# A decoder layer in which VectorE takes two instructions of the cross-attention in the other order

## The chip, the cores and the metric

The kernel runs on one core of a Trainium2 chip. The metric is the device time of one execution in microseconds (us). Three runs of the kernel before took 3787.0, 3793.76 and 3797.38 us; their median is 3793.76 us.

## The reference

One decoder layer over x of 16 batches x 224 rows x 512, all in fp32. Three parts are added to x one after the other, each computed from a layer norm of x:

```python
x = x + self_attention(layernorm(x))          # 16 heads of 64, causal, rotary
x = x + cross_attention(layernorm(x), ctx)    # 16 heads of 32, 750 context rows of 384 a batch
x = x + experts(layernorm(x))                 # 8 experts, top 2, capacity 560 rows each, F = 2048
```

The change lies in the cross-attention:

```python
q = (x @ Wq).reshape(B, N, 16, 32);  k, v = (context @ Wk), (context @ Wv)   # likewise in heads
scores = einsum('bhid,bhjd->bhij', q, k) * 32 ** -0.5    # a mask over the 750 keys
out = einsum('bhij,bhjd->bhid', softmax(scores), v)      # then all heads side by side
return out @ Wo                                          # added to x: the "residual" below
```

## The kernel before, in words

The layer runs in three stages: self-attention, cross-attention, experts. Within a stage each engine has a program of its own, a fixed list of instructions that it takes strictly in this order; engines wait for one another by semaphores. No planner sorts them: the order stands in the code.

**Steps and sub-steps.** The cross-attention goes through 16 batches; batches 2 to 14 are a loop, the first two and the last are written out. A batch has four steps (g = 0 to 3), one for each group of four heads, and a step has four sub-steps (j = 0 to 3), one a head. In each sub-step PE (TensorE) computes the scores of 112 rows (half h = 0) against all keys, then some other work (`first_gap`), then the scores of the other 112 rows (h = 1), then more other work (`second_gap`). VectorE takes the row maximum of each (L1605, `maximum`), followed by its own `first_gap` and `second_gap`. The scores are computed a second time with the maximum subtracted, for the step before (L1170), ScalarE takes the exponential (L1440), POOL sums it (L1029 to L1035), PE multiplies by the values (L1183).

**Units and banks.** The other work comes in units: a projection or a transposition that fills one bank of PSUM, from which another engine takes the result. Three banks (`x_pj`) are handed out in turn in the order of a written list. For a whole batch it has 45 units; those of step g = 2 are

```python
"K30 M1_2 O1 K31 V14 V15 C00 C10 Q0 C20 M0_2 C01 Q1 C11"
```

so O1 and V15 share a bank (three places apart), as do K31 and C00, and each must wait until the unit ahead of it in its bank has been taken out (`pj_free`). The units that matter here:
- **K30, K31**: the keys of the next group of heads, columns 0 to 373 and 374 to 749. ScalarE writes a rounded ("high") copy (L1383), VectorE the difference ("low" part, L1599, `low_k`); a product of high and low parts then takes three matmuls (L32 to L34). When both parts of both halves are there, SP copies them into the stationary tiles `k_st` with three or four transfers a head (L953 to L957, `place_k`).
- **O0, O1**: the output projection of the batch before, 112 rows each (L1123). VectorE adds it to the residual `x_xres` (L1629, `residual`).
- **V14, V15**: parts of the values (L32 to L34 with `wv`, 9 matmuls each), taken out by ScalarE (L1387).
- **C00, C10**: transpositions of the next batch's context (L1089).
- **M0, M1**: the transposed maxima, written into partitions 96 to 98 of `q_st` by ScalarE (high) and VectorE (low, L1611, `low_max`).

**The place of the change** is step g = 2, sub-step j = 1, in VectorE's `second_gap`. PE's order there is: scores of j = 1 h = 0, K31, scores h = 1, sums of the exponentials (L1195), V14, V15, scores of j = 2. VectorE's order is: maximum h = 0, low part of M1_2, maximum h = 1, low part of K31, residual of O1, maximum of j = 2. SP's order is: the copies of K31's step (`place_k(t + 3, ...)`), the store of the finished residual, the queries of the next batch; later in the next body the context, the mask row and the keys of step 1.

Of the kernel before, what the change touches and what calls it, by code (L numbers as in the profile page):

```python
# [790 lines left out]
def unit_of(b, name):  # L791

    if isinstance(b, int) and b == -1:
        return Bank(U_PRE.index(name), 0, 0)
    start = len(U_PRE)
    if isinstance(b, int) and b == 0:
        return Bank(start + U_FIRST.index(name), 0, 0)
    start += len(U_FIRST)
    if isinstance(b, int) and b == 1:
        return Bank(start + U_SECOND.index(name), 0, 0)  # L800
    start += len(U_SECOND)
    if isinstance(b, int) and b == B - 1:
        return Bank(start + (B - 3) * len(UNITS) + U_LAST.index(name), 0, 0)
    return Bank(start - 2 * len(UNITS) + UNITS.index(name), b, len(UNITS))
# [20 lines left out]
def cross_attention(nc, x1, x1n, ctx, cmask, w_o, router_w, cst, x2, rows_w, logits, op):  # L825

    with ExitStack() as outer:
# [9 lines left out]
        with ExitStack() as c:  # L837
# [49 lines left out]
            def below(n, k):  # L887
                return isinstance(n, int) and n < k
# [17 lines left out]
            with nc.Block() as block:  # L906
# [660 lines left out]
                def _(dve):  # L1567
                    def any_key(b):

                        dve.wait_ge(mask_step, 3 * b + 1)  # L1570
                        dve.tensor_reduce(valid[:], mk[:], AX.X, ALU.max).then_inc(valid_done, 1)
# [4 lines left out]
                    def low_x(b, h):  # L1576
                        u, name = unit_of(b, f"X{h}"), f"X{h}"
                        hi_ready(b, name)
                        cols = slice(h * HT, (h + 1) * HT)
                        dve.tensor_tensor(xT[1][:, :, cols], pj[u.bank][:, 0:4 * HT].rearrange("p (k t) -> p k t", k=KD),  # L1580
                                          xT[0][:, :, cols].bitcast(F32), ALU.subtract).then_inc(pj_free[u.bank], 1)

                    def low_ctx(b, k, s):
                        u = unit_of(b, f"C{k}{s}")
                        hi_ready(b, f"C{k}{s}")
                        cols = slice(s * HALF, (s + 1) * HALF)
                        dve.tensor_tensor(cT[1][:, k, cols], pj[u.bank][:, 0:HALF], cT[0][:, k, cols].bitcast(F32),
                                          ALU.subtract).then_inc(pj_free[u.bank], 1)

                    def low_q(b, i):  # L1590
                        u = unit_of(b, f"Q{i}")
                        hi_ready(b, f"Q{i}")
                        dve.scalar_tensor_tensor(qT[1][:, i, :], pj[u.bank][:, 0:T], valid[:, 0:1], qT[0][:, i, :].bitcast(F32),
                                                 ALU.mult, ALU.subtract).then_inc(pj_free[u.bank], 1)
# [12 lines left out]
                    def low_max(u, n, g, i):  # L1607

                        dve.wait_ge(m_high, n)
                        rows = q_st[96:99, 4 * g + 2 * i:4 * g + 2 * i + 2, :]  # L1610
                        dve.scalar_tensor_tensor(rows, pj[u.bank][96:99, 0:2 * T].rearrange("p (j t) -> p j t", j=2),  # L1611
                                                 less[96:99, 0:1], rows.bitcast(F32), ALU.mult, ALU.add).then_inc(pj_free[u.bank], 1)

                    def invert(t, i):

                        dve.wait_ge(z_full, t + 1)
                        cols = slice(i * HT, i * HT + HT)
                        dve.reciprocal(rz[:, cols], psZ[:, cols]).then_inc(recip, 1)

                    def out_y(t, g, out=None):  # L1620
                        dve.wait_ge(recip, 2 * t + 2)
                        if out is not None:
                            dve.wait_ge(pj_full, out.n + 1)
                        dve.tensor_tensor(yT[:, g, :], psY, rz[:], ALU.mult).then_inc(y_ready, 1)

                    def residual(u, b, h):
                        dve.wait_ge(xres_loaded, 16 * b + 16)
                        dve.wait_ge(pj_full, u.n + 1)
                        dve.tensor_tensor(xres[:, h, :], pj[u.bank][0:HT, :], xres[:, h, :], ALU.add).then_inc(pj_free[u.bank], 1)  # L1629
# [35 lines left out]
                    def body(b, first, last):  # L1665
                        t = 4 * b
                        old = not below(b, 2)

                        def U(name):
                            return unit_of(b, name)  # L1670

                        def first_gap(g, j):
                            n, prev, pprev, gp = t + g, not (first and g == 0), not (first and g < 2), (g + 3) % 4
                            if j == 0:
                                if g == 1 and not last:
                                    low_x(b, 1)
                                elif g == 2 and not first:
                                    residual(U("O0"), b - 1, 0)
                            elif j == 1:
                                if prev:  # L1680
                                    low_max(U(f"M1_{g}"), 2 * n, gp, 1)
                            elif j == 2:
                                if pprev:
                                    invert(n - 2, 0)
                            else:
                                if g == 0:
                                    low_q(b, 3)
                                if pprev:
                                    out_y(n - 2, (g + 2) % 4, U("O1") if g == 2 and not first else None)
                                if g == 2 and not last:  # L1690
                                    low_ctx(b, 2, 0)
                                low_max(U(f"M0_{g}"), 2 * n + 1, g, 0)

                        def second_gap(g, j):
                            n, pprev = t + g, not (first and g < 2)
                            nxt, ng = not (last and g == 3), (g + 1) % 4
                            if j == 0:
                                if nxt:
                                    low_k(b, ng, 0)
                                if g == 3 and not last:  # L1700
                                    low_ctx(b, 2, 1)
                                if g == 3 and not first:
                                    router_norm(b - 1, 0, [U(f"O{h}") for h in range(2)])
                            elif j == 1:
                                if nxt:
                                    low_k(b, ng, 1)
                                if g == 2 and not first:
                                    residual(U("O1"), b - 1, 1)
                            elif j == 2:
                                if g == 0:  # L1710
                                    low_q(b, 2)
                                elif g == 2 and not last:
                                    low_ctx(b, 0, 0)
                                    low_ctx(b, 1, 0)
                                elif g == 3 and not first:
                                    router_norm(b - 1, 1)
                                if pprev:
                                    invert(n - 2, 1)
                                if g == 2 and not last:
                                    low_q(b, 0)  # L1720
                            else:
                                if g == 0 and not last:
                                    low_x(b, 0)
                                elif g == 1 and not last:
                                    any_key(b + 1)
                                elif g == 2 and not last:
                                    low_ctx(b, 0, 1)
                                    low_q(b, 1)
                                    low_ctx(b, 1, 1)
                                elif g == 3 and not first:  # L1730
                                    router_norm(b - 1, 2)

                        for g in range(4):
                            for j in range(4):
                                maximum(t + g, j, 0)
                                first_gap(g, j)
                                maximum(t + g, j, 1)
                                second_gap(g, j)
# [759 lines left out]
```

## Time and profile before

| | |
|---|---|
| median of three runs | 3793.76 us |
| the profiled execution | 3791.84 us, span 3790.1 us |
| PE busy | 3640.3 us, 96% of the span |
| PE's weight loads busy | 3139.0 us, 83% |
| VectorE busy | 2363.4 us, 62% |
| ScalarE busy | 1730.3 us, 46% |
| POOL busy | 1299.5 us, 34% |
| the cross-attention | from about 1090 to 2460 us |
| one batch of its loop | 83.7 us |

The span is the time from the first to the last instruction of one execution. A busy share is an average over stages; what an edit is worth is read from the waits of the stage in which it lies. PE is shown twice: its matmuls (PE) and the loading of their weights (PEld), which runs beside them and sets their pace here. An engine is idle ahead of an instruction either for want of something from another engine, which the profile names behind an arrow, or for "issue", where it names nothing. A line number is that of the kernel before.

### The profile page before, as it was taken

The numbers are of one execution on the slowest core, as the hardware profiler recorded it, in microseconds if no ns is written. First come the engines' busy times: TensorE is split into PE (matmuls) and PEld (weight loads), VectorE is DVE, ScalarE is ACT, GpSimd is POOL, SyncE is SP. The second block draws the span as 40 slices with busy tenths as digits, with TensorE's granted clock in tenths as the row PEclk, the third lists the DMA queues.
The fourth block names the chain that finished last, engine by engine and source line by source line (L and its number), as shares of the span: only waits on it lengthen the run. The fifth ranks groups of instructions, "written<-read, shape, count | busy, mean of one in ns | idle before, by whom it ended". The sixth has DMA issues, their size and how long they took to land. (4 is left out here: it accounts for less than half of the span.)

```text
span 3790.1 us, 84211 instructions
## 1 busy us (share of the span) xinstructions
PE 3640.3 (96%) x28244; PEld 3139.0 (83%) x28244; DVE 2363.4 (62%) x5547; ACT 1730.3 (46%) x4277; POOL 1299.5 (34%) x1385
## 2 busy tenths in 40 slices
PE   7999999999979999999999999849999999999999
PEld 6888888888868888888888888639999899989998
DVE  6888888888856666666666666567434334334343
ACT  4555555555535555555555555413333333333332
POOL 1333333333315556666555566510101101011010
PEclk9999999999979999999999999869999999999999
DMA  4222222222243443444434443223323333233232
GB/s 125 60 54 63 53 63 53 63 53 63 61 128 98 107 107 104 107 115 107 118 102 105 110 105 96 68 67 95 120 84 120 106 98 123 84 120 119 87 107 70
DMA packets 315057, 349.72 MB, mean 92 GB/s; under 512 B 45308, under 2 KB 232036, under 8 KB 314884
## 3 DMA queue, kind: packets, MB, share of 16 engines
q1 hardware_dynamic: 305796, 318.26, 30.3%
q0 software_dynamic: 9088, 29.17, 2.4%
q8 instruction: 106, 1.74, 0.2%
q14 instruction: 67, 0.55, 0.0%
HBM read 183.23 MB, written 38.91 MB: 59 GB/s over the span
## 5 line engine op out<-in xcount | busy, mean ns | idle before, releaser
L1605 DVE TENSOR_REDUCE x_mx<-x_psS 112x1 f32<-112x752 f32 x512 | 479.9, 937 | 388.3 <-PE x_psS L1158 384.5
L2401 DVE TENSOR_TENSOR hid<-e_psU,act_g 128x280 f32<-128x280 f32 x256 | 115.2, 450 | 626.2 <-PE e_psU L34 615.9
L1440 ACT ACTIVATE x_pt<-x_psE 125x448 f32<-125x448 f32 x768 | 389.2, 541 | 231.3 <-PE x_psE L1170 221.8
L1029 POOL TENSOR_TENSOR part<-x_pt 125x448 f32<-125x448 f32 x255 | 292.0, 1145 | 514.6 <-ACT x_pt L1440 505.8
L2027 POOL DMA_INDIRECT out<-ex_y,sidx x40 | 39.8, 994 | 1014.2 <-DVE ex_y L2435 1006.5
L611 POOL TENSOR_TENSOR qks<-qks,cos 128x448 f32<-128x448 f32 x128 | 147.8, 1155 | 676.6 <-DMA qks<-qk 676.6
L1158 PE MATMUL x_psS<-k_st,q_st 97*112 97x376 f32 x1024 | 287.5, 362 | 22.9 <-DMA k_st<-mk 15.0
L32 PE MATMUL e_psG<-ex_hi,g_hi 128*128 128x280 f32 x1024 | 303.9, 297 | 4.2 <-DVE ex_lo L2394 2.2
L32 PE MATMUL pj<-xT_hi,win_hi 128*128 128x224 f32 x1024 | 302.8, 296 | 1.4 <-DVE xT_lo L651 1.3
L32 PE MATMUL e_psU<-ex_hi,u_hi 128*128 128x280 f32 x1024 | 298.2, 291 | 0.4 <-DVE hid L2401 0.3
L1031 POOL TENSOR_TENSOR part<-part,x_pt 125x448 f32<-125x448 f32 x255 | 291.7, 1144 | 20.0
L34 PE MATMUL e_psG<-ex_hi,g_lo 128*128 128x280 f32 x1024 | 298.4, 291 | 0.0
L34 PE MATMUL e_psU<-ex_hi,u_lo 128*128 128x280 f32 x1024 | 297.7, 291 | 0.0
L33 PE MATMUL e_psG<-ex_lo,g_hi 128*128 128x280 f32 x1024 | 297.1, 290 | 0.0
L33 PE MATMUL e_psU<-ex_lo,u_hi 128*128 128x280 f32 x1024 | 297.0, 290 | 0.0
L2186 ACT ACTIVATE act_g<-e_psG 128x280 f32<-128x280 f32 x256 | 103.3, 404 | 423.5 <-PE e_psG L34 417.0
L34 PE MATMUL pj<-xT_hi,win_lo 128*128 128x224 f32 x1024 | 282.3, 276 | 0.0
L33 PE MATMUL pj<-xT_lo,win_hi 128*128 128x224 f32 x1024 | 281.7, 275 | 0.0
L1170 PE MATMUL x_psE<-q_st,k_st 99*125 99x224 f32 x1536 | 262.8, 280 | 6.4 <-ACT x_pt L1440 4.0
L1170 PEld LDWEIGHTS x_psE<-q_st,k_st 99*125 99x125 f32 x1536 | 235.9, 190 | 16.0 <-ACT x_pt L1440 11.6
L2190 ACT ACTIVATE hid_hi<-hid 128x280 fp32r<-128x280 f32 (+1 forms) x256 | 107.0, 418 | 288.5 <-DVE hid L2401 288.5
L674 DVE CUSTOM_DVE_ANT_0 pr<-psS,mask 112x112 f32<-112x112 f32 (+1 forms) x512 | 139.4, 329 | 128.8 <-issue 67.6
(301 smaller groups left out, 10888.3 us busy)
## 6 DMA issues: line engine op xcount, KB each, us to landing
k_st<-kT SPq DMA_DIRECT2D x768, 93.8 KB, 2.2
raw_g<-in_L_ffn_wg SPq DMA_DIRECT2D x128, 256.0 KB, 2.8
raw_u<-in_L_ffn_wu SPq DMA_DIRECT2D x128, 256.0 KB, 2.8
raw_d<-in_L_ffn_wd SPq DMA_DIRECT2D x128, 256.0 KB, 2.8
qks<-qk SPq DMA_DIRECT2D x512, 56.0 KB, 2.0
q_st<-qT SPq DMA_DIRECT2D x384, 56.0 KB, 2.0
ctxt<-in_ctx SPq DMA_DIRECT2D x16, 1125.0 KB
xt<-in_x SPq DMA_DIRECT2D x16, 448.0 KB, 3.7
```

What stands on the lines that cost most here:

```text
L32: pe.matmul(out, lh, rh, start=first, stop=False)
L33: pe.matmul(out, lh, rl, start=False, stop=False)
L34: return pe.matmul(out, ll, rh, start=False, stop=last)
L611: pool.tensor_tensor(qks[i][:], qks[i][:], cos[:].unsqueeze(1).to_broadcast((P, 2, T)), ALU.mult)
L674: m = dve.tensor_tensor_reduce(pr[par][:, hd, to:to + n], psS[hd][0:HT, to:to + n], mask[:, h, 0:n], -SD ** -0.5, -NEG, ALU.add, ALU.min, ...
L1029: pool.tensor_tensor(part[:], pt[j][:, 0, :], pt[j][:, 1, :], ALU.add).then_inc(parted, 1)
L1031: pool.tensor_tensor(part[:], part[:], pt[j][:, 2, :], ALU.add).then_inc(parted, 1)
L1158: m = pe.matmul(psS[0:HT, s, 0:376], q_st[0:97, head, h * HT:(h + 1) * HT], k_st[4 * (g % 2) + j][0:97, SHALF[s]], start=True, stop=True)
L1170: m = pe.matmul(psE[(j + i) % 2][0:KR, s * T:(s + 1) * T], k_st[4 * (g % 2) + j][0:99, r * KR:(r + 1) * KR], q_st[0:99, 4 * g + j, :], sta ...
L1440: act.activation(pt[j][:, i, :], psE[(j + i) % 2][0:KR, 0:2 * T], ACT.Exp, scale=XD ** -0.5).then_inc(exp_done, 1)
L1605: dve.tensor_reduce(mx[:, j, h:h + 1], psS[0:HT, :, 0:376], AX.XY, ALU.max).then_inc(s_taken, 1)
L2401: dve.tensor_tensor(h[ring][:, halves[s]], psU[:, 0:CH], act_g[i][:, halves[s]], ALU.mult).then_inc(S["mul"], 1)
```

## The change

In `second_gap` of VectorE, sub-step j = 1, the residual of O1 is placed ahead of the low part of the keys, not behind it. It concerns step g = 2 of batches 1 to 15; in the other steps only the low part is there. No other engine's program is touched, and no instruction is added or removed.

```diff
                             elif j == 1:
+                                if g == 2 and not first:
+                                    residual(U("O1"), b - 1, 1)
                                 if nxt:
                                     low_k(b, ng, 1)
-                                if g == 2 and not first:
-                                    residual(U("O1"), b - 1, 1)
                             elif j == 2:
```

## Rows read from the trace of the kernel before

**Rows 1.** The page: busy us (share of the span) and instructions of each engine.

```profile
PE 3640.3 (96%) x28244; PEld 3139.0 (83%) x28244; DVE 2363.4 (62%) x5547; ACT 1730.3 (46%) x4277; POOL 1299.5 (34%) x1385
```

**Rows 2.** One batch's length, busy PE, PEld, DVE, ACT, POOL; PEclk; DMA share, GB/s.

```profile
1560.00:1643.90 83.90, 82.54 (x718) 69.57 (x714) 56.32 (x82) 47.61 (x96) 49.98 (x62) 1.00 0.41 109
```

**Rows 3.** Waits of PE's weight loads, cross-attention: us in total, times, longest.

```profile
PEld x_pj L32 <- DVE x_xres L1629: 9.9, 15, 0.7
```

**Rows 4.** VectorE's timeline: start, us, line, operation, [idle before <- releaser].

```profile
1569.56 0.69 DVE L1611 SCALAR_TENSOR_TENSOR q_st<-x_pj,x_less,q_st 3x448 fp32r<-3x448 f32 x1
1571.15 0.94 DVE L1605 TENSOR_REDUCE x_mx<-x_psS 112x1 f32<-112x752 f32 x1 [0.89 <-PE x_psS L1158]
1572.12 0.55 DVE L1599 TENSOR_TENSOR kT<-x_pj,kT 128x376 fp32r<-128x376 f32 x1
1572.59 0.68 DVE L1629 TENSOR_TENSOR x_xres<-x_pj,x_xres 112x512 f32<-112x512 f32 x1
1575.04 0.94 DVE L1605 TENSOR_REDUCE x_mx<-x_psS 112x1 f32<-112x752 f32 x1 [1.77 <-PE x_psS L1158]
```

**Rows 5.** Timeline of PE's weight loads from V14 to V15.

```profile
1572.36 0.18 PEld L33 LDWEIGHTS x_pj<-wv,cT 128*125 128x125 f32 x1
1572.47 0.18 PEld L34 LDWEIGHTS x_pj<-wv,cT 128*125 128x125 f32 x1
1573.32 0.18 PEld L32 LDWEIGHTS x_pj<-wv,cT 128*125 128x125 f32 x1 [0.66 <-DVE x_xres L1629]
```

**Rows 6.** VectorE's timeline at O0's residual, batch 5 and (last two) batch 15.

```profile
1556.70 0.94 DVE L1571 TENSOR_REDUCE valid<-mk 128x1 f32<-128x750 f32 x1
1561.89 0.94 DVE L1605 TENSOR_REDUCE x_mx<-x_psS 112x1 f32<-112x752 f32 x1 [4.26 <-PE x_psS L1158]
1562.75 0.68 DVE L1629 TENSOR_TENSOR x_xres<-x_pj,x_xres 112x512 f32<-112x512 f32 x1
...
2399.28 0.94 DVE L1605 TENSOR_REDUCE x_mx<-x_psS 112x1 f32<-112x752 f32 x1 [5.22 <-PE x_psS L1158]
2400.25 0.69 DVE L1629 TENSOR_TENSOR x_xres<-x_pj,x_xres 112x512 f32<-112x512 f32 x1
```

**Rows 7.** Weight loads of C00 and C10, the next users of the two banks.

```profile
1575.19 0.65 PEld L1089 LDWEIGHTS x_pj<-ident,ctxt 125*128 125x128 f32 x6
```

**Rows 8.** SP's queue: copies of K31's step, queries, first copy of the next batch.

```profile
1572.94 0.51 SPq L953 DMA_DIRECT2D k_st<-kT  x1
...
1578.10 0.59 SPq L955 DMA_DIRECT2D k_st<-kT  x1
1580.56 0.51 SPq L953 DMA_DIRECT2D k_st<-kT  x1
...
1589.89 2.52 SPq L968 DMA_DIRECT2D q_st<-qT  x4
1595.66 0.56 SPq L953 DMA_DIRECT2D k_st<-kT  x1
```

**Rows 9.** Mask row's copy and the scores behind it, batches 6 and 3.

```profile
L957 SPq DMA_DIRECT2D k_st<-mk x1: 847/847/847, 1615.2 to 1615.2; - x1
DMA to landing us min/median/max: 7.1/7.1/7.1
...
1622.42 0.60 PE L1158 MATMUL x_psS<-k_st,q_st 97*112 97x376 f32 x2
...
DMA to landing us min/median/max: 8.5/8.5/8.5
...
1369.61 0.45 PEld L1158 LDWEIGHTS x_psS<-k_st,q_st 97*112 97x112 f32 x2 [2.61 <-issue]
```

**Rows 10.** VectorE's timeline: O1's residual in batches 2 to 4.

```profile
1317.69 0.68 DVE L1629 TENSOR_TENSOR x_xres<-x_pj,x_xres 112x512 f32<-112x512 f32 x1
...
1405.15 0.68 DVE L1629 TENSOR_TENSOR x_xres<-x_pj,x_xres 112x512 f32<-112x512 f32 x1
...
1488.87 0.68 DVE L1629 TENSOR_TENSOR x_xres<-x_pj,x_xres 112x512 f32<-112x512 f32 x1
```

## The prediction

> **What bounds the kernel now.** I read the page first, then three views of the cross-attention stage. On the page PE is busy 96% of the span, VectorE 62% [rows 1]. The stretch view makes it plain for this stage: in a batch of the loop (83.9 us) PE is busy 82.54 us at a granted clock of 1.00 (2.4 GHz), VectorE 56.32 us [rows 2]. So an edit of VectorE's order is worth only what TensorE waits for VectorE, and the reader is to look for that wait. It is in the waits of PE's weight loads: `PEld x_pj L32 <- DVE x_xres L1629`, 9.9 us in 15 times, 0.66 each [rows 3]. L1629 is `residual`; the waiting load is the first of V15, which must write the bank in which the second output half (O1) lies.
>
> The two timelines of one such place, batch 5 in step g = 2, sub-step j = 1, show it in detail. VectorE runs the second maximum at 1571.15, K31's low part at 1572.12, the residual at 1572.59 for 0.68 us, so to 1573.27 [rows 4]. PE loads weights every 0.11 to 0.12 us while it does V14, its last load starts at 1572.47 and ends at 1572.65, and V15's first starts at 1573.32: 0.67 us of idle, ended 0.05 us behind the residual's end [rows 5]. Unhindered it would have come at 1572.59, so 0.73 us are lost here.
>
> **The change part by part.** No instruction is added or removed. In 15 batches (1 to 15) two VectorE instructions change places: the 112x512 residual add goes ahead of the 128x376 low part of K31.
>
> *The residual starts earlier.* Its data are there: O1's product was queued on PE before K31, and the loaded residual has already served the first half at 1562.75 [rows 6]. It must still follow the second maximum (start 1571.15), and how closely is the one unknown. Two rows bound it. The first half's residual started 0.86 us behind its maximum in batch 5 (1561.89 to 1562.75), but 0.97 us behind it in batch 15 (2399.28 to 2400.25) [rows 6]. K31's low part, in the very slot that the residual takes over, also starts at 0.97 (1571.15 to 1572.12) [rows 4]. I take 0.97: it is what this slot shows, and the instruction ahead of the maximum is here the low part of the maxima (L1611) [rows 4], while in batch 5's first half it was L1571 [rows 6], which batch 15, having no next batch, doesn't run: there too it is L1611. The residual then runs from 1572.12 for 0.69 us [rows 6] to 1572.81, and V15's first load starts 0.05 us later, at 1572.86, instead of at 1573.32: 0.46 us gained. With 0.86 it is 1572.01 + 0.68 + 0.05 = 1572.74, 0.58 us gained; the end of the range is the whole 0.73, if the wait went entirely.
>
> The Trainium skill has a rule for the two offsets (VectorE: DVE Perf Modes, section "Two Vector instructions with no wait between them"): an instruction is held until all earlier ones are finished if an input from SBUF begins in another group of 32 partitions than the last SBUF input read before it. L1611 reads its SBUF input in partitions 96 to 98, the maximum reads no SBUF, and the residual begins at partition 0, so by the rule it is held here and in batch 15's first half, and not held behind L1571, which begins at partition 0. The trace agrees: 0.97 is the maximum's 0.94 us and 0.03 more, 0.86 is less than its duration [rows 6]. Without holding the sum would be 15 x 0.58 = 8.7 us, with it 6.9.
>
> *K31's low part starts later.* It moves from 1572.12 to between 1572.72 and 1572.81: the residual's 0.69, or 0.60 if the next instruction overlaps its end by 0.08 to 0.09, as the residual overlaps the low part today (0.55 long, followed at 0.47) [rows 4]. It ends by 1573.36, against 1572.67. Three things wait for it.
> - VectorE's own next instruction, the maximum of j = 2, has 1.77 us of idle ahead of it [rows 4]. The new pair ends at most 0.09 us later than the old one (no overlap), and the maximum comes 0.46 earlier, so at least 1.2 us stay. Everything behind it on VectorE keeps its distance to PE.
> - PE's next user of K31's bank, the turning of the context (C00), loads at 1575.19 [rows 7], and would at 1574.73: 1.4 us behind the low part's end.
> - SP's queue places K31 with 12 copies, the first at 1572.94, 0.27 us behind the low part [rows 8]. It would start at 1573.63 at the latest, 0.69 late. The first nine go out back to back (to 1578.10 + 0.59 = 1578.69) and then the queue idles to 1580.56, since the last slot is still being read by PE [rows 8]. Late, the ninth ends at 1579.38; the tenth is released 0.46 earlier than now, at 1580.10. So 0.7 us of cover are left, and the store of the residual and the placing of the queries behind it in the queue start with PE, 0.46 earlier. Without that cover each batch would pay its 0.69. The first of these copies is read by the scores that begin step 3, many us later (on PE after the values that are queued at the end of step 2).
>
> *V15 comes earlier.* Its eviction by ScalarE, the scores of j = 2 and their maximum are all released by PE in this place, and shift by 0.46. The next wait of PE on another engine that could eat the gain is on a VectorE chain that starts with that same maximum at 1575.04, so it shifts too. POOL plays no part: nothing of PE's here waits for it.
>
> *Does the shift last?* Only a clock of its own could take it back. SP's long run of copies for the next batch starts at 1595.66 behind an idle queue [rows 8], released by K01's low part, hence by PE. The second chain that hangs on it is tight, though: the copy of the mask row for step g = 1 is issued at 1615.2 and lands 7.1 us later, at 1622.3; PE's scores start at 1622.42 [rows 9]. But both chains start after the edited place, so their distance does not change.
>
> **The sum.** 15 x 0.46 = 6.9 us. Against the profiled execution: 3791.84 - 6.9 = 3784.9 us. That execution lies 1.9 us under the median of the runs, 3793.76, so for the median I say 3786.9 us.
>
> **Rivals.**
> - *A: the residual is not held, or the wait goes entirely.* For it: 0.86 stands at the first half's residual [rows 6]. Against it: the slot's own 0.97 [rows 4]. 15 x 0.58 = 8.7 us, 3785.1; with the whole wait gone, 15 x 0.73 = 11.0 us, 3782.8.
> - *B: the gain is taken back at the mask row's landing*, in step g = 1 of the next batch. For it: a margin of 0.1 us [rows 9]. Against it: SP's idle before 1595.66, by which that chain follows PE [rows 8]. If it held its own pace nothing would be left: 3793.8.
> - *C, the other side: the landing comes late in more batches.* Batch 3 shows the price. Its copy took 8.5 us, and PE's scores started at 1369.61 after 2.61 us of idle [rows 9]. From residual to residual that batch took 1405.15 - 1317.69 = 87.46 us, the next 83.72 [rows 10]: 3.74 us lost. With n more such batches the sum is -6.9 + 3.74 n; it turns slower from n = 2 (3794.4), and n = 5 gives 3805.6. It would decide if a PE that waits less meets the landings 0.1 us or more earlier than now. Against it: one such batch in 14 and the argument that both chains shift together.
> - *D: the change does nothing*, because V15's load would be held by something else at 1573.3. Nothing else ends there: V14's loads are in even pace up to 1572.47 and the wait ends on the residual [rows 5].
>
> **How the numbers follow.** The forecast 0.65; A 0.16; B and D together 0.11; C 0.08. The runs of before lie between 3787.0 and 3797.38, so a median can be off by 3 or so either way; a difference of under 0.3% (11.4 us) can't be told from no change. The forecast alone: 3782 to 3792. The range that takes in A's end and B is 3780 to 3795; C from three late batches on and the far side of A with a low run are left out. Faster by over 0.3% needs A's end or a lucky run on top of A: 0.14. Slower by over 0.3% needs C with n = 5 or more: 0.03. Within 0.3%: 0.83.
>
> **What would show it.** Behind the second maximum of g = 2, j = 1: residual at +0.97, K31's low part 0.6 to 0.7 behind that. The wait of V15's load on the residual: 1572.86 - 1572.65 = 0.21 us each, 3.1 us in 15 times, instead of 9.9. The distance between two residuals of the loop: 83.26 us instead of 83.72. SP's idle before the tenth copy of K31 shrinks from 1.9 to 0.7 us. It is wrong if V15's load is released before 1572.8 or after 1572.9 on that scale, if C00's load waits for K31's low part, if SP's tenth copy follows the ninth without a pause, or if the shift is gone by the next batch's step 1.

## The result, and the profile after

The changed kernel took 3782.64 us (median of 22 runs, 3775.26 to 3790.87) beside 3787.61 us for the kernel before in the same comparison (22 runs, 3782.25 to 3797.38). The ratio is 0.9986, with a 95% interval of 0.9980 to 0.9992: 5.3 us faster, 3.0 to 7.6. Two later comparisons gave 0.9981 (0.9972 to 0.9990) and 0.9982 (0.9973 to 0.9990). Over all three the mean of the changed kernel's 45 runs is 3782.3 us and that of the 70 runs of before beside them 3788.7: 6.4 us. The forecast was 6.9, and a median of 3786.9.

VectorE's timeline of the changed kernel at the place of [rows 4], batch 5:

```profile
1565.03 0.69 DVE L1611 SCALAR_TENSOR_TENSOR q_st<-x_pj,x_less,q_st 3x448 fp32r<-3x448 f32 x1
1566.61 0.94 DVE L1605 TENSOR_REDUCE x_mx<-x_psS 112x1 f32<-112x752 f32 x1 [0.89 <-PE x_psS L1158]
1567.59 0.69 DVE L1629 TENSOR_TENSOR x_xres<-x_pj,x_xres 112x512 f32<-112x512 f32 x1
1568.19 0.54 DVE L1599 TENSOR_TENSOR kT<-x_pj,kT 128x376 fp32r<-128x376 f32 x1
1570.05 0.94 DVE L1605 TENSOR_REDUCE x_mx<-x_psS 112x1 f32<-112x752 f32 x1 [1.31 <-PE x_psS L1158]
```

The residual starts 0.98 us behind the maximum, and ends at 1568.28; K31's low part follows it by 0.60. From this maximum to the next one it is 3.44 us, where [rows 4] had 3.89. PE's weight loads beside it, the answer to [rows 5]:

```profile
1567.94 0.18 PEld L34 LDWEIGHTS x_pj<-wv,cT 128*125 128x125 f32 x1
1568.33 0.18 PEld L32 LDWEIGHTS x_pj<-wv,cT 128*125 128x125 f32 x1 [0.21 <-DVE x_xres L1629]
```

And the wait summed over the stage, the answer to [rows 3]:

```profile
PEld x_pj L32 <- DVE x_xres L1629: 3.1, 15, 0.2
```

The idle time of the load has shrunk from 0.66 to 0.21 us, 15 times. SP's queue, as in [rows 8]:

```profile
1569.01 0.51 SPq L953 DMA_DIRECT2D k_st<-kT  x1
...
1574.17 0.59 SPq L955 DMA_DIRECT2D k_st<-kT  x1
1575.58 0.51 SPq L953 DMA_DIRECT2D k_st<-kT  x1
```

The first copy of K31's step starts 2.40 us behind the maximum, not 1.79; the ninth ends at 1574.76 and the queue still idles 0.82 us ahead of the tenth, so the delay ends there. O1's residual in batches 2 to 4, as in [rows 10]:

```profile
1316.19 0.69 DVE L1629 TENSOR_TENSOR x_xres<-x_pj,x_xres 112x512 f32<-112x512 f32 x1
...
1401.04 0.69 DVE L1629 TENSOR_TENSOR x_xres<-x_pj,x_xres 112x512 f32<-112x512 f32 x1
...
1484.33 0.69 DVE L1629 TENSOR_TENSOR x_xres<-x_pj,x_xres 112x512 f32<-112x512 f32 x1
```

The later distance is 83.29 us, for 83.72 before. The earlier one, with the late landing of batch 3, is 84.85 for 87.46. Of these 2.6 us the edit has 0.4; in the other 2.2 it has no part, and they are why the spans of the two traces (3781.0 and 3790.1) differ by 9.1 us, more than the runs do.

Cut at the maxima that open batches 1 and 15, the executions profiled so far read as follows. "Late landings" are batches 4 to 14 whose step 1 begins over 18.30 us behind step 0, and the us over 18.26 that all eleven lose; "rest" is from batch 15 to the end, with batch 15's own residual in it, and the last column how long TensorE's granted clock was at its lower level (1.2 GHz) in the rest, its fall in the last 3 us left out.

| trace | batch 0 at | batches 1 to 15 | late landings | batch 3 | rest | lower level |
|---|---|---|---|---|---|---|
| before | 1101.6 | 1174.8 | 3, 0.6 us | 87.4 | 1431.4 | 92 |
| before, again | 1105.6 | 1173.9 | 9, 2.1 us | 85.6 | 1431.1 | 89 |
| changed | 1101.2 | 1167.0 | 7, 1.8 us | 84.8 | 1430.8 | 89 |
| changed, again | 1105.9 | 1169.2 | 8, 2.4 us | 86.6 | 1432.2 | 96 |
| changed, third | 1102.0 | 1168.3 | 6, 1.2 us | 86.8 | 1433.1 | 96 |

What batch 3 loses has two parts. Its step 1 begins 1.6 to 2.6 us late in these five traces. In three of them (the first of before, the second and third of the changed kernel) TensorE's granted clock was also at its lower level for 3.4 us as PE went on, and the batch lost 1.1 to 1.5 us more; in the other two there was neither.

### The profile page after: what moved, and what is told of

It is laid out like the page before. It is cut to its first block and busy times, and to the rows that moved or that the text cites. A ratio compares the mean times of both kernels' runs of the same rounds, so it can differ in the third digit from the quotient of the medians.

```text
span 3781.0 us, 84211 instructions
## 1 busy us (share of the span) xinstructions
PE 3636.5 (96%) x28244; PEld 3136.9 (83%) x28244; DVE 2363.4 (63%) x5547; ACT 1731.8 (46%) x4277; POOL 1298.8 (34%) x1385
```

## The experiments

All of them are edits of the changed kernel unless another is named. Six of the twelve were repeats, made to tell the edit from an execution's chance.

**The changed kernel again, twice.**

> The changed kernel once more, as the yardstick for the runs beside it. In its first trace the wait of V15's load on the residual fell from 9.9 to 3.1 us and the distance between residuals by 0.46 us a batch, so 6.9 us should be gained in every execution; measured were 5.3 (3.0 to 7.6). Theory 1 (the gain is 6.9 and what is missing is the chance of where copies land late in step 1): the trace shows 3.1 us of wait again, a batch distance of 83.2 to 83.3 us wherever the mask row's copy lands in time, and late landings that differ from trace to trace; time 3.0 to 7.6 us under before. Rival (the earlier PE meets the landings earlier, so they cost more after the change in each execution): step 1 begins more than 18.3 us behind step 0 in more batches than in the kernel before, where it did in three of eleven.

> The changed kernel, a third trace and more runs. Late landings so far (step 1 over 18.30 us behind step 0, batches 4 to 14): old order 3 and 9 traces' batches, for 0.6 and 2.2 us; new order 7 and 8, for 1.8 and 2.4. Theory (chance from execution to execution): anything from 3 to 9, 0.5 to 2.5 us. Rival (the new order meets more of them): 7 or more again. Time 3778 to 3785 us.

3780.98 us and 3782.77 us, ratios as above. Both traces show 3.1 us for the wait and looped batches of 83.2 to 83.3 us wherever the landing isn't late. The edit's gain in the loop is in every trace.

**The kernel before again.**

> The kernel before, profiled once more, for its late landings in step 1. So far, counted as step 1 beginning more than 18.30 us behind step 0, batches 4 to 14: 3 in the kernel before, for 0.6 us in all; 7 and 8 in the two traces of the changed one, for 1.8 and 2.4 us. If that is chance from execution to execution (theory 1): any count from 2 to 9 here, and batch 3 loses 1.6 to 2.6 us or more. If the old order really meets them less (rival): 4 or fewer, and under 1 us in all.

Its one run took 3796.12 us, more than any of the 16 beside it (3785.64 to 3793.56). Nine late landings, 2.1 us, and batch 3 at 85.6 us. With 3 and 9 in the old order and 7, 8 and 6 in the new, that the changed kernel meets more of them isn't shown; five traces are too few to exclude a part of a microsecond.

**Why 0.97 and not 0.86.** A tiny copy between the low part of the maxima and the second maximum:

```diff
                                     low_max(U(f"M1_{g}"), 2 * n, gp, 1)
+                                if g == 2 and not first:
+                                    dve.tensor_copy(touch[:], ident[:, 0:1])
```

> The changed kernel with one tiny copy on VectorE, from partition 0 on to partition 0 on, between the low part of the maxima and the second maximum of g = 2, j = 1, in time in which VectorE idles. Theory (the residual starts late because the last SBUF input read before it, that of the low part of the maxima, began at partition 96): the residual starts 0.86 us behind the maximum, not 0.97; V15's load waits 0.10 us, not 0.21, in 15 batches, and 1.6 us more are gained. Rival (0.97 belongs to this slot, by its waits and its register work): it stays at 0.97 and the wait at 3.1 us, no gain. The theory is the rule of the Trainium skill, VectorE: DVE Perf Modes, section Two Vector instructions with no wait between them.

VectorE's timeline of this kernel in batch 4, and the load of V15 beside it (the line numbers are one higher):

```profile
1484.04 0.15 DVE L1684 COPY x_touch<-ident 128x1 f32<-128x1 f32 x1
1484.90 0.94 DVE L1606 TENSOR_REDUCE x_mx<-x_psS 112x1 f32<-112x752 f32 x1 [0.71 <-PE x_psS L1159]
1485.75 0.68 DVE L1630 TENSOR_TENSOR x_xres<-x_pj,x_xres 112x512 f32<-112x512 f32 x1
...
1486.22 0.18 PEld L34 LDWEIGHTS x_pj<-wv,cT 128*125 128x125 f32 x1
1486.49 0.18 PEld L32 LDWEIGHTS x_pj<-wv,cT 128*125 128x125 f32 x1
```

The same residual in the same slot now starts 0.85 us behind the maximum, ahead of its end, and the load idles 0.09 us. So the offset is not the slot's own. That it goes by where the last SBUF input begins, and not by the mere presence of one more instruction, is borne out by rows without the copy. In the kernel before, 122 instructions of five kinds follow L1611 and a maximum, and all start 0.97 us behind that maximum. Another 59 have inputs that begin at partition 0 and follow a maximum behind an instruction whose inputs begin there too (the residual, L1571 or the low part of x), and all start at 0.86. In the next experiment K31's low part, in its old slot but now behind the residual and the maximum, starts at 0.86 as well. That agrees with the rule of the Trainium skill weighed in the prediction (VectorE: DVE Perf Modes, section "Two Vector instructions with no wait between them"). The time, 3778.62 us (0.9979, 0.9970 to 0.9989), is 2.4 us under the changed kernel's beside it, with scatter enough to hide it; the batches without a late landing took 83.13 to 83.20 us, so of 0.12 us a batch some 0.05 came through; what took the rest back isn't shown.

**The residual one place earlier.** It goes ahead of the second maximum:

```diff
                             elif j == 1:
                                 if prev:
                                     low_max(U(f"M1_{g}"), 2 * n, gp, 1)
+                                if g == 2 and not first:
+                                    residual(U("O1"), b - 1, 1)
```

> The changed kernel with O1's residual one place earlier still: ahead of the second maximum of g = 2, j = 1, behind the low part of the maxima. Theory (V15's wait is the whole of what the order costs, 0.73 us a batch before the change, and VectorE has 0.89 us of idle there): the wait of PE's load on the residual vanishes, the maximum is not delayed by more than 0.05 us, the batch takes 83.0 us; against the changed kernel 15 x 0.27 = 4.0 us are gained, against before 11.0. Rival (the residual of 0.69 us does not fit between the low part of the maxima, which ends 0.90 us ahead of the maximum, and the maximum): the maximum starts up to 0.2 us late, and the scores of j = 2 with it; no gain against the changed kernel.

Its VectorE timeline in batch 4:

```profile
1481.41 0.69 DVE L1611 SCALAR_TENSOR_TENSOR q_st<-x_pj,x_less,q_st 3x448 fp32r<-3x448 f32 x1
1482.13 0.69 DVE L1629 TENSOR_TENSOR x_xres<-x_pj,x_xres 112x512 f32<-112x512 f32 x1
1482.99 0.94 DVE L1605 TENSOR_REDUCE x_mx<-x_psS 112x1 f32<-112x752 f32 x1 [0.17 <-PE x_psS L1158]
1483.85 0.54 DVE L1599 TENSOR_TENSOR kT<-x_pj,kT 128x376 fp32r<-128x376 f32 x1
1486.16 0.94 DVE L1605 TENSOR_REDUCE x_mx<-x_psS 112x1 f32<-112x752 f32 x1 [1.77 <-PE x_psS L1158]
```

It fits: the maximum still waits for PE (0.17 us), from maximum to maximum it is 3.17 us, and the wait of V15's load is gone from the list. Batches without a late landing took 82.98 to 83.04 us, about 0.2 less than in the changed kernel. The run time, 3779.12 us (0.9977, 0.9968 to 0.9987), is 1.9 us under the changed kernel's beside it, for 4.0 expected; with ten runs that scatter by 4 us it can't be told from either.

**K31's low part really late.** It goes behind the first maximum of j = 2:

```diff
                             elif j == 2:
+                                if g == 2:
+                                    low_k(b, 3, 1)
                                 if pprev:
                                     invert(n - 2, 0)
```

> The changed kernel with the low part of K31 moved on, behind the first maximum of j = 2: some 2.9 us later than in the changed kernel. It shows what K31's low part costs when it is really late. By my account C00's turning on PE, due at 1570.2 on the changed kernel's scale (1574.7 on the scale of before), then waits for it: the low part ends 1.4 us behind the maximum's start (0.86 + 0.54), the maximum starts 0.15 us ahead of C00's load, so 1.2 to 1.3 us of wait in each of 16 batches, 20 us slower than the changed kernel; SP's first copy of K31 starts 2.9 us later, and its tenth follows the ninth without a pause. Rival (the late copies cost as well): over 30 us, with PE waiting at step 3 for copies of k_st. Second rival (C00 has other cover): under 5 us.

3803.3 us (1.0037, 1.0023 to 1.0050): 21 us above the changed kernel's mean, for 20 expected. From PE's waits in this kernel:

```profile
PE x_pj L1089 <- DVE kT L1599: 17.4, 15, 1.3
```

C00's turning waits 1.2 us in each batch, as worked out, though 15 times and not 16, since batch 15 has no next context to turn. Batches without a late landing took 84.5 to 84.6 us, 1.3 more than in the changed kernel. SP's tenth copy of K31's step followed the ninth without a pause, and no wait of PE at step 3 came of that. So the bank is what limits K31's low part: the change under study pushes it back by 0.6 us and leaves 1.5 of the 2.5 us that it ended ahead of C00's load (the load having come 0.45 earlier too). This experiment moved it 2.7 us further, 1.3 beyond that cover, and about that much was paid. Its copies have far more cover.

**The late landings.** SP issues the next batch's context behind step 1's copies:

```diff
-                            load_ctx(b + 1)
+                            load_mask(b + 1)
                         place_k(t + 1, b, 1, [unit_of(b, "K10"), unit_of(b, "K11")])
+                        if not last:
+                            load_ctx(b + 1)
```

> The changed kernel, but SP issues the next batch's context (1125 KB) behind the copies of step 1's keys and mask row, not ahead of them; the mask's own load stays ahead. Theory (the copies for step 1 land 7 us after issue because they stand behind the context's load, and some land behind the moment when PE wants them): the mask row's copy for j = 0 lands after 2 to 3 us, batch 3 loses its extra 1.6 to 3.7 us and the other batches their 0.1 to 0.7, every looped batch takes 83.2 us; 3 to 5 us gained, and runs that scatter less than the 10 to 15 us of now. Rival A (the mask's broadcast with its small packets is what delays them): landing stays at 5 us or more, no gain. Rival B (the context now delays the queries or step 2's keys): waits of PE on these copies, in step 2, and a loss.

> The changed kernel with the context's load behind step 1's copies, once more. Theory (as for the old order's run): 3771 to 3775 us again, loop of 1164.3 us from batch 1 to batch 15, low level for 80 to 84 us from batch 15 on. Rival (drawn anew): 3771 to 3787, with a low level of other length.

3773.29 us (0.9964, 0.9950 to 0.9977), and again 3771.61 us (0.9951, 0.9938 to 0.9964), between 8 and 11 us under the changed kernel. The copy of the mask row behind which PE used to wait, to compare with [rows 9]; under it the mask's own broadcast, in this kernel and in the changed one (columns: issues, KB each, median us from issue to landing):

```profile
DMA to landing us min/median/max: 1.9/1.9/1.9
```

```profile
mk<-in_mask_BxS_bf SPq DMA_DIRECT2D x1, 93.8 KB, 3.0
```

```profile
mk<-in_mask_BxS_bf SPq DMA_DIRECT2D x2, 93.8 KB, 12.8
```

The copy lands in 1.9 us for 7.1, the broadcast in 3.0 for 12.8: both had stood behind the context's 1125 KB. The copy is issued 10.5 us behind the batch's first maximum in both kernels, so only its landing has changed. In two traces no batch is late, batch 3 takes 83.25 and 83.14 us, and batch 0 is 3.4 to 4.4 us shorter as well. Of rival B something came, but only once: the queries behind the load were issued more slowly (10.8 us for the twelve, 7.7 before), and at the start of batch 0's step 2 PE stood still for 2.7 us until they and the keys had landed. In the loop it waited for neither. So the 3.74 us that batch 3 lost in the kernel before came from a transfer's place in a queue, with the low clock behind the wait.

**The old order without late landings.** The same edit of SP, on the kernel before.

> The kernel before, in its old order (low part of the keys, then the residual), with nothing but the context's load issued behind step 1's copies. It pairs with the changed kernel that has the same edit (3773.29 us, looped batches of 83.25 to 83.28 us, no late landing). Theory (the edit itself is worth 0.46 us a batch, 6.9 us in all, whatever the landings do): batches of 83.7 us, a wait of 9.9 us on the residual, and 6.9 us more than that kernel, 3780.2 us; about 8.7 us less than the kernel before. Rival (part of the edit's gain comes only by way of the landings): a difference other than 6.9 by more than 2.

> The old order with the context's load behind step 1's copies, once more. It came 13.5 us above its pair with the new order, though its batches are only 0.41 us longer (5.7 us from batch 1 to batch 15); the other 7.8 us lie after the loop and in the scatter. In its trace batch 15 and the way to the experts took 189.2 us, in the pair's 180.8, and TensorE's clock was at its lower level for 98.8 us from batch 15 on, in the pair's 82.0. Theory (where the low level of the clock begins and ends behind the loop is fixed for a kernel by the time at which it gets there): 3784 to 3789 us again, low level for 95 us or more from batch 15 on. Rival (it is drawn anew in each execution): a trace with 82 to 89 us, and a median under 3783.

3786.82 us (0.9990, 0.9981 to 0.9999), and again 3783.15 us (0.9982, 0.9973 to 0.9991). The expected time of 3780.2 us was missed by 3 to 7 us. In the loop the two orders differ as the theory has it: looped batches of 83.67 us (median) against 83.26 and 83.21, and from batch 1 to batch 15 1170.0 and 1169.9 us against 1164.3 and 1163.5, 6.1 us for the 14 residuals between, 0.44 each. But the run times differ by 11.5 us (means 3784.6 of 22 runs and 3773.0 of 11, uncertain by 0.5 and 1.0), and by 10.0 in the one comparison in which both kernels ran. The rest of the execution, where only batch 15's residual (0.4 us) differs between these kernels, took this long: first the stretch from batch 15 to the end of the old order's first trace, then that of the new order's (columns of [rows 2]).

```profile
2350.44:3788.00 1437.56, 1361.02 (x9423) 1222.98 (x9421) 650.81 (x1337) 483.53 (x1044) 191.89 (x208) 0.96 0.32 97
```

```profile
2344.98:3769.30 1424.32, 1352.93 (x9423) 1218.61 (x9421) 649.12 (x1337) 483.76 (x1044) 192.42 (x207) 0.97 0.33 98
```

13.2 us apart, with the clock at its lower level for 99 and 82 us. The second traces moved towards each other: 1431.5 us with 89 in the old order, 1432.4 us with 96 in the new. So neither theory stands as it was put: the rest isn't fixed for a kernel, since the repeats differ by 6 and 8 us, and whether it leans one way in the old order isn't settled by two traces each. The new order's second trace is of the slowest of its six runs (3780.55 us, the others 3768.73 to 3775.93), so it may hide such a lean. Some 5 us of the 11.5 stay unexplained. Without the context's move nothing of the kind is to be seen: the rest took 1431.1 and 1431.4 us in the old order, 1430.8 to 1433.1 in the new, and the run times differ by 6.4 us, which the residuals account for.

**Both: residual in the first gap, context later.**

> The changed kernel with the residual in the first gap, ahead of the second maximum, and the context's load behind step 1's copies. Theory (V15's remaining wait and the late landings are two separate losses): 15 x 0.27 = 4.1 us less than with the context's load alone, 3769.2 us; batches of 82.98 us and no late landing. Rival (they share a cover): less than 2 us.

> The same with the residual in the first gap, once more. Its loop was 4.5 us shorter than with the context's load alone, but its median the same. In its one trace batch 0 began 4.3 us later (1106.4 for 1102.1), with 6.8 us more at the lower clock before it, though nothing differs between the kernels there. Theory (that is the execution's chance): a start of batch 0 near 1100 to 1103 in some executions, and a median of 3769 to 3771. Rival (the low stretches take the gain back in each execution): 3773 again.

3773.15 us (0.9957, 0.9944 to 0.9971) and 3769.62 us (0.9946, 0.9930 to 0.9961). From batch 1 to batch 15 it took 1159.8 and 1160.1 us, 3.9 us less than with the context's load alone, as expected, and no landing was late. In the run times only 1.6 us of it are to be seen (means 3771.4 and 3773.0 of 11 runs each, uncertain by 1.3 and 1.0). The expectation of an earlier start was not met: batch 0 began at 1105.1 in the repeat too, behind 44 us of stretches with the clock at its lower level, as in three traces of other kernels; where it began by 1102.2, these were 31 to 38 us. This is the best kernel of the study, 0.43% and 0.54% faster than the one before in its two comparisons, of which the change under study is a third or so.

## Why the prediction was right

- *The wait and its price.* Right in each term: 0.97 to 0.98 from maximum to residual, 0.69 for it, 0.05 to PE's load; the wait 0.21 us each, 3.1 in all, as forecast.
- *Held or not.* The choice of 0.97 over 0.86 was right, and for the reason given: with one instruction between, the same residual started at 0.85. Rival A was a real alternative, worth 0.12 us a batch at the load.
- *K31's low part.* It follows the residual by 0.60, the lower of the two figures. SP's cover was 0.82 us, forecast 0.7; C00 did not wait. The experiment that moved it 2.7 us further showed what lies behind the cover: 1.2 us a batch.
- *The shift lasts.* The distance between residuals is 83.2 to 83.3 us for a forecast 83.26. Rival B would have left 83.7.
- *The landings.* The tight spot was read rightly from [rows 9]: the mask row's copy lands close to PE's need, late in 3 to 9 of batches 4 to 14, by 0.8 us at most, in each of the five traces. That the change leaves it alone is borne out as far as five traces can, where the counts of the two orders overlap; a second batch as dear as batch 3, as rival C has it, stood in none of them. The price that it took from batch 3, 3.74 us, was not the landing's alone: 1.1 us of it went with the low clock, and in the other four traces the batch lost 1.6 to 3.6.
- *The size.* 6.9 us forecast, 5.3 (3.0 to 7.6) measured, 6.4 over all comparisons. The two pairs of traces without late landings give 0.44 us a residual for 0.46, 6.5 us for the 15. What is left is the scatter of the executions. It has three sources in the traces: late landings (3 to 6 us with batch 3), the start of batch 0 (up to 5 us), and the rest from batch 15 on (2 us among the five traces of these two kernels, 13 among all). A traced execution is no typical one: it was the slowest one in five of the twelve sets of runs.
- *The time.* 3786.9 us forecast, 3782.64 measured. The starting point was off: the median of three runs, 3793.76, lay 6.2 us above that of 22, 3787.61, twice the 3 us allowed for, and the two medians measured lie 5.0 apart, not 6.9, which took 1.9 of it back. That the result still fell within 3782 to 3792, by 0.6 us, was luck. It even lies next to rival A's far end (3782.8), which the traces rule out. The time alone would have pointed to the wrong mechanism.

## What to carry to other kernels

On an engine that isn't the bottleneck, look for the one wait that the bottleneck has on it, and put what ends that wait ahead of what has cover; then reckon the cover of what was pushed back at each of its readers, transfers too. A gain of 0.2% can be read from the trace's distances long before the run times show it: compare the distance between the same two instructions in many batches, and take landings, start and end apart. Take the starting time from many runs too: a median of three was 6 us off here, as much as the change is worth. A large transfer ahead of small urgent ones in one queue can cost more than the reordering of an engine, so look at the time to landing of each small copy whose reader starts right behind it.

## What the runs showed of the hardware

- A VectorE instruction may start ahead of the end of the one before it or only behind it, 0.85 to 0.86 against 0.97 us behind the same 0.94 us maximum, and an added 0.15 us copy that reads from partition 0 turned the later into the earlier. In the kernel before all 122 instructions behind one that reads from partition 96 and a maximum started at 0.97.
- A load of 1125 KB ahead in SP's queue kept a copy of 2.9 KB from landing for 7.1 us; with the load issued behind the copy that was 1.9. The issue of the broadcast right behind the load took 3.6 to 3.9 us, and 0.38 ahead of it.
- From batch 15 to the end the same instructions, but for batch 15's residual, took 1424 to 1438 us, with the clock at its lower level for 82 to 99 us; the shortest and the longest go with the least and the most of it. The executions differ there more than this change is worth.
- In three of five traces the granted clock went to its lower level for 3.4 us when PE went on behind its wait of 1.9 to 2.6 us for batch 3's copy, and the batch lost 1.1 to 1.5 us beyond the wait. In the other two, behind 1.6 and 2.0 us, the clock stayed up.
